# The middle batches of both attention passes written out, with all waits on constants, in place of a loop on the engines

## What is computed

```python
# pass A: cross attention, 16 heads of 32, relative position bias
x = x + tanh(g_xattn[0]) * xattn(layernorm(x), ctx, ctx, mask, ...)
#   Q, K, V = query @ Wq + bq, key @ Wk + bk, value @ Wv + bv      (16 heads of 32)
#   scores = Q K^T / sqrt(32) + rel_bias[:, clip(q - k)];  masked;  softmax;  @ V;  @ Wo + bo
# pass B and C: x = x + tanh(g_ffn[0]) * ffn(layernorm(x))
#   pass B, inside ffn: h = h + attention(rmsnorm(h))    causal, 16 heads of 64 (32 plain, 32 rotary),
#                        keys and values out of a latent of 64 features
#   pass C, inside ffn: h + moe(rmsnorm(h))              one shared expert, the best 2 of 8 routed
```

## Time and profile before

| | |
|---|---|
| median of 3 runs | 2403.45 us (2398.34 to 2407.27) |
| the profiled execution | 2406.51 us, its span 2404.7 us |
| TensorE matmul busy | 2139.2 us, 89% of the span |
| VectorE busy | 1507.1 us, 63% |
| GpSimd busy | 1365.8 us, 57% |
| ScalarE busy | 1175.7 us, 49% |
| mean granted TensorE clock | 0.955 |

### The profile page before, as it was taken

One profiled execution on the slowest core, in us unless ns is written; L12 is line 12 of the kernel. 1 busy time (PEld: TensorE's weight loads), 2 busy tenths in 40 slices (PEclk: granted clock), 3 DMA queues, 4 the chain that ended last, 5 costly groups with the idle time before them and its releaser, 6 DMA issues. The chain is left out here.

```text
span 2404.7 us, 49921 instructions
## 1 busy us (share of the span) xinstructions
PE 2139.2 (89%) x12672; PEld 974.7 (41%) x12673; DVE 1507.1 (63%) x4218; ACT 1175.7 (49%) x2316; POOL 1365.8 (57%) x1452
## 2 busy tenths in 40 slices
PE   3899999999999963899999999999985797899997
PEld 1333333333333311344444444444432443455554
DVE  3788888887888843566566566565544678344443
ACT  3355555555555442355545455454544474455554
POOL 4267677677677670265655565565651565455554
PEclk7999999999999986899999999999997899899999
DMA  5413323232232203443534344352414566666665
GB/s 176 146 60 102 104 81 117 71 106 91 93 107 76 84 5 130 146 121 117 152 93 135 119 135 124 99 155 89 140 43 137 112 153 133 107 114 114 113 110 90
DMA packets 222936, 264.57 MB, mean 110 GB/s; under 512 B 39192, under 2 KB 165004, under 8 KB 222388
## 3 DMA queue, kind: packets, MB, share of 16 engines
q1 hardware_dynamic: 197612, 212.79, 29.1%
q0 software_dynamic: 22976, 48.38, 11.5%
q10 hardware_dynamic: 2072, 0.28, 0.1%
HBM read 162.12 MB, written 86.80 MB: 104 GB/s over the span
## 5 line engine op out<-in xcount | busy, mean ns | idle before, releaser
L497 ACT ACTIVATE a_pt<-a_bank 128x512 f32<-128x512 f32 x512 | 305.1, 597 | 371.0 <-DVE a_bank L604 359.4
L1384 DVE CUSTOM_DVE_ANT_0 b_bank<-b_bank,b_tri 128x256 f32<-128x256 f32 (+3 forms) x512 | 253.9, 498 | 312.0 <-PE b_bank L1521 307.8
L615 DVE CUSTOM_DVE_ANT_0 a_bank<-a_bank,a_strip 128x512 f32<-128x512 f32 x512 | 354.1, 692 | 6.9 <-PE a_bank L758 4.3
L1169 POOL TENSOR_TENSOR b_acc<-b_acc,b_pt 128x256 f32<-128x256 f32 (+2 forms) x384 | 272.0, 726 | 102.4 <-ACT b_pt L1258 84.3
L407 POOL TENSOR_TENSOR a_acc<-a_acc,a_pt 128x512 f32<-128x512 f32 x256 | 317.2, 1272 | 8.0 <-ACT a_pt L497 4.3
L604 DVE TENSOR_TENSOR a_bank<-a_bank,a_band 128x256 f32<-128x256 f32 (+1 forms) x512 | 206.8, 405 | 136.6 <-PE a_bank L745 135.3
L1258 ACT ACTIVATE b_pt<-b_bank 128x256 f32<-128x256 f32 (+2 forms) x384 | 144.0, 383 | 204.7 <-PE b_bank L1505 194.1
L745 PE MATMUL a_bank<-a_q_stack,a_k_stack 128*128 128x512 f16 x512 | 196.8, 386 | 16.2 <-ACT a_pt L497 12.0
L758 PE MATMUL a_bank<-a_k_stack,a_q_stack 97*128 97x512 f16 x512 | 196.0, 383 | 3.8 <-DVE a_low L615 3.7
L1851 POOL DMA_INDIRECT out_dram<-c_z,c_to_row x72 | 114.1, 1585 | 137.1 <-DMA out_dram<-c_z,c_to_row 102.3
L1503 PE MATMUL b_bank<-b_q_stack,b_k_stack 96*128 96x256 f16 (+3 forms) x512 | 155.8, 304 | 10.6 <-issue 5.4
(11 more groups left out here) (346 smaller groups left out, 5449.4 us busy)
## 6 DMA issues: line engine op xcount, KB each, us to landing
b_q_stack<-qk_rows SPq DMA_DIRECT2D x192, 128.0 KB, 2.7
a_q_stack<-qk_rows SPq DMA_DIRECT2D x96, 128.0 KB
a_k_stack<-qk_rows SPq DMA_DIRECT2D x96, 128.0 KB
b_k_stack<-qk_rows SPq DMA_DIRECT2D x96, 128.0 KB, 2.6
a_sums<-in_x SPq DMA_DIRECT2D x34, 256.0 KB, 3.4
qk_rows<-a_qk_hi SPq DMA_DIRECT2D x64, 128.0 KB, 1.7
qk_rows<-a_qk_lo SPq DMA_DIRECT2D x64, 128.0 KB, 1.8
out_dram<-a_sums SPq DMA_DIRECT2D x32, 256.0 KB, 2.0
```

The source lines that it names most:

```text
L497: nc.scalar.activation(pt[:, n % SLOTS, :], st_bank[n % 2][:], ACT.Exp).then_inc(exped, 1)
L615: nc.vector.tensor_tensor_reduce(out=max_bank[step % 2][:], in0=max_bank[step % 2][:], in1=strip[:, g * HG + hh, at:at + S], scale=-1.0, s ...
L1169: nc.gpsimd.tensor_tensor(sums_of, sums_of, probs(n), ALU.add).then_inc(pooled, 1)
L1384: nc.vector.tensor_tensor_reduce(out=max_bank[step % 2][:, 0:w], in0=max_bank[step % 2][:, 0:w], in1=tri[:, at:at + w], scale=-1.0, scalar ...
```

## The change

In both passes the loop of `over` becomes a loop of the program text: the six middle batches stand one behind the other in every engine's program, b is a number in each, and so every count and every address is a constant. Pass C is not touched, nor the order of the work within a batch.

```diff
--- before.py
+++ after.py
@@ -233,9 +233,8 @@
 
             body("first", -1, 1)
             body("zero", 0, 0)
-            with eng.Fori(0, ROUNDS // 2) as i:
-                for u in range(2):
-                    body("steady", i * 2 + (1 + u), (1 + u) % 2)
+            for b in range(1, B - 1):
+                body("steady", b, b % 2)
             body("last", B - 1, (B - 1) % 2)
             body("end", B, B % 2)
 
```

## The result

| | median, us | runs |
|---|---|---|
| before | 2402.58 (2398.34 to 2407.27) | 7 |
| after | 2392.50 (2390.08 to 2396.44) | 7 |

The ratio is 0.996, with a 95% interval of 0.9947 to 0.9972: faster by 0.4%, some 10 us, where 14.5 us (0.6%) had been forecast. It is inside the 0.5% for which I had given 0.33, not beyond it, for which I had given 0.61.

A forecast was written before the change was run, and what follows sets the result against it. TensorE was taken to bound the middle batches. Jumps 13.7, constants 0.8 and new code 0 sum to 14.5 us: 2406.5 profiled becomes 2392.0, or 2389.0 us on the median's footing, range 2378 to 2402.

The forecast's parts named there:

- What bounds it, and where the gain lies: Middle batches of A and B: TensorE bounds them; the excess sits at the loop's jumps back behind batches 2 and 4.
- The jump, 13.7 us: Four jumps back, two a pass, on TensorE: late instruction fetch goes, saving 3.70 us in A and 9.98 in B.
- The prediction's own bound, 10 to 18 us: Four loop edges of A and B: the gain another execution may give, as edges lie between 1.6 and 5.8 us.
- One count is enough: At the jumps back: all five engines jump, but all stand still behind TensorE, so the price is counted once.
- The waits on constants, 0.8 us: Middle batches: wait values become constants, not registers; nothing on TensorE, 0.8 us taken from ScalarE's hops, upper bound 2.1.
- The 0.07 us: ScalarE's exponentials in the loop: start 0.47 us after VectorE's addition starts, 0.40 with constants; the difference would go.
- The new code at nothing: Six written-out batches a pass, four extra copies each fetched new: cost taken as 0, judged from batch 0.
- stalls at each block of TensorE's straight code: Rival, TensorE's six copies: 37 new packets at 1.40 us each give 52 us, 2441 us; chance 0.06.
- the gap is not the jump's: Rival, loop edges: the gap stays, perhaps another engine's hand-over; at most 0.8 us comes, 2402.7 us; chance 0.12.
- constants bring more: Rival, middle batches' residual waits of 29.9 us: half goes with the register instructions, 15 us, 2374.8 us; chance 0.12.
- slower: Rival, TensorE's straight code: it stalls at each new block of instructions, 2441 us; chance 0.06.
- 0.49 of the 0.70: Whole kernel: of the forecast's chance 0.70, 0.49 was for a gain beyond 12 us (0.5%), 0.21 within.

The follow-up runs named there:

- the hint: Kernel before, loops and registers kept, with a prefetch hint for the jump back set on all five engines; ratio 0.9959 to the kernel before.
- slot 0: Kernel before, loops kept, TensorE's program padded so each attention loop's body begins at the head of a 256-instruction block; 2411.4 us, ratio 1.004.
- the short loops added: Changed kernel plus a three-round loop around one no-operation behind batches 2 and 4, all engines, both attentions; 2399.1 us, 0.9975 of the kernel before.

## Why the prediction was right or wrong

**What bounds it, and where the gain lies:** right. Shown by the batches after, and by the hint, which brings the gain with the loop kept. In A the batches came a little under the 101.2 to 101.4 us forecast (101.07 to 101.20).

**The jump, 13.7 us:** the mechanism right, the size too high: of the terms of the sum this one is off. It was read off one execution. A second of the same kernel gives 10.4, and the kernel with TensorE's loop alone has gaps of 1.87, 1.53, 3.20 and 2.61 us, in another order of size. The mean of the two, 12.0, and 1.0 of constants would have been 13. The prediction's own bound, 10 to 18 us for another execution, held 10.1 only just, and the two later measurements (9.8 and 8.2 by the medians, 7.7 and 8.2 by the ratios) are under it. What parts 13 us in the traces from 8 to 10 in the plain runs stays open. One reading is that the profiler makes late fetches later; the middle batches of plain executions can't be seen, and slot 0, where the plain time is above the profiled one, speaks against so simple a rule. The other is chance in the batches 0, whose spread of 3 to 6 us is as large as the difference.

**One count is enough:** right for the sum, wrong as a picture in A, where VectorE and ScalarE come from their jumps as late as TensorE.

**The waits on constants, 0.8 us:** 1.0 measured, hint against written out, one profile each. TensorE's share is none, as costed. The 0.07 us went on ScalarE in full (0.47 to 0.39), and what TensorE kept waiting for was VectorE, as read. The 1.0 is net of the new delays of the next paragraph.

**The new code at nothing:** right on TensorE, not quite on VectorE. In batch 3 of B VectorE starts a maximum 0.35 us late, in the profiles of the changed kernel (three), of both runs with pass C written out, and of TensorE alone looping. With the short loops added it moves to batch 5 (101.77 us). It is not the only one. First that one, with the same maximum in batch 2 of B ahead of it, in the first profile of the changed kernel, 56.4 and 56.8 us behind the cuts of their batches:

```profile
1247.46 0.70 DVE L1382 CUSTOM_DVE_ANT_0 b_bank<-b_bank,b_tri 128x512 f32<-128x512 f32 x1 [1.90 <-PE b_bank L1519]
...
1349.26 0.70 DVE L1382 CUSTOM_DVE_ANT_0 b_bank<-b_bank,b_tri 128x512 f32<-128x512 f32 x1 [2.24 <-PE b_bank L1519]
```

Eight of VectorE's instructions in the middle batches start 0.15 to 0.37 us later behind their predecessor than the same instruction does in most batches. Counted from the start in VectorE's recorded instructions they are numbers 1087, 2879, 3007, 3392, 3519, 3775, 3903 and 4416, which lie whole multiples of 128 apart, to one. The packets of queue q14 are of 8192 bytes, and 128 instructions make one if an instruction has the 64 bytes that 16,384 bytes for 256 of them give on q8. So these are most likely the edges of VectorE's own blocks, in straight code. Most are covered; three reach TensorE, as 0.13 us in batch 3 of A, 0.35 in batch 3 of B and 0.15 in batch 6 of B. As a rival, stalls at each block of TensorE's straight code, it is refuted: none is seen, and the traffic fell.

**The rivals:** "the gap is not the jump's" is refuted by the hint; "constants bring more" by 1.0 us; "slower" by the ratio, though its mechanism exists in small on VectorE.

**The chances:** with the size read from one execution and a boundary of 12 us, putting 0.49 of the 0.70 beyond it was too sure. The spread of the edges' prices was in the trace (1.64 and 2.06 for two passes over the same jump in A) and should have pulled the centre down as well as widened it, since the profiled execution lay 3.1 us above the median.

## What to carry to other kernels

A loop on the engines whose body is too long to be at hand cost each engine 2.6 to 4.8 us from branch to first instruction here. Of this the bound engine showed 1.6 to 3.4 us as idle time at every jump back, and it lost up to 6 with a stall behind it and a lower clock. So look for "issue" on the bound engine at every nth batch edge, and count the engines that jump, since the second latest may cost as much. A wait label on the gap can mislead: look when the engine named had ended. A prefetch hint on the back edge brought as much as writing the rounds out, without a longer program. Take such a price from several executions, and expect it to change when anything ahead of the loop changes its length.

## What the runs showed of the hardware that I had not expected

- A jump's price hangs in part on where its target lies in a block: at 24 instructions from the end, a second stall of 1.4 us in A and 3.7 us in B follows, eight matmuls behind the first.
- Code ahead of a loop seems to set a part of the loop's price: with pass A written out, pass B's untouched edges cost 2.9 us in all and not 7.1 or 10.0 (one profile; the cause argued, not shown).
- The loops fetched more instruction bytes than the written-out code, 3.11 MB against 2.32, with 49921 and 43597 instructions run; with the hint it was 2.78.
- A short loop of three rounds, taken branches and all, cost nothing on TensorE while it had matmuls to do.
- All five engines are late behind a far branch, by 2.6 to 4.8 us in the kernel before, and VectorE, whose code comes in pieces of 8192 bytes, is up to 0.37 us late at some edges of these pieces even in straight code.
